# Attention sum of a GRU recurrence: from the exponential's own sum to a second ScalarE pass, with its products inside the gate products

## What is computed

```python
def step(h, x_t):
    proj = h @ W
    score = jnp.einsum('bsh,bh->bs', enc_hiddens, proj)     # 77 context rows
    attn = jax.nn.softmax(score, axis=-1)
    context = jnp.einsum('bs,bsh->bh', attn, enc_hiddens)
    inp = jnp.concatenate([x_t, context], axis=-1)
    gx = inp @ kernel + bias
    gh = h @ recurrent_kernel
    z = jax.nn.sigmoid(xz + hz)
    r = jax.nn.sigmoid(xr + hr)
    cand = jnp.tanh(xh + r * hh)
    h_new = z * h + (1.0 - z) * cand
    return (h_new, h_new)
```

## Time and profile before

| | |
|---|---|
| median of 3 runs | 3198.2 us (3195.73 to 3201.64) |
| the profiled execution | 3192.87 us, its span 3190.7 us |
| mean granted TensorE clock | 0.967 of full |
| TensorE products, weight loads | 2753.8 us (86%), 1822.2 us (57%) |
| VectorE | 2173.4 us (68%) |
| ScalarE | 1711.2 us (54%) |
| GpSimd | 931.2 us (29%) |
| first and last exponential of the recurrence | 1035.1 and 3021.4 us from the start |

### The profile page before, as it was taken

One profiled execution on the slowest core, in us unless ns is written; L12 is line 12 of the kernel. 1 busy time (PEld: TensorE's weight loads), 2 busy tenths in 40 slices (PEclk: granted clock), 3 DMA queues, 4 the chain that ended last, 5 costly groups with the idle time before them and its releaser, 6 DMA issues. The chain is left out here.

```text
span 3190.7 us, 131407 instructions
## 1 busy us (share of the span) xinstructions
PE 2753.8 (86%) x54380; PEld 1822.2 (57%) x54382; DVE 2173.4 (68%) x8164; ACT 1711.2 (54%) x5751; POOL 931.2 (29%) x1930
## 2 busy tenths in 40 slices
PE   5999999787678999898999898999989777777769
PEld 3666666575445555565665565666556444444449
DVE  5666666773442888688888787777778766666663
ACT  3666666533443666575776575666667433333311
POOL 0000000030010566354666354555535200000011
PEclk8999999998888999999999999999999999999979
DMA  4000000000011000010000010000000000000012
GB/s 137 5 5 5 7 5 5 1 1 10 16 32 41 7 14 30 3 43 4 10 14 27 16 31 3 10 10 12 21 17 23 3 4 3 3 3 3 3 46 61
DMA packets 38727, 55.45 MB, mean 17 GB/s; under 512 B 5934, under 2 KB 25336, under 8 KB 38008
## 3 DMA queue, kind: packets, MB, share of 16 engines
q1 hardware_dynamic: 36344, 42.46, 4.3%
q0 software_dynamic: 1792, 4.62, 0.6%
HBM read 42.45 MB, written 4.62 MB: 15 GB/s over the span
## 5 line engine op out<-in xcount | busy, mean ns | idle before, releaser
L2016 POOL TENSOR_TENSOR gru_terms<-gru_states,gru_signs 128x8 f32<-128x8 f32 x512 | 103.6, 202 | 1196.5 <-DVE gru_states L2222 1088.5
L1937 ACT ACTIVATE gru_p<-gru_ps_sg,gru_negmax 128x78 f32<-128x78 f32 x512 | 166.9, 326 | 361.2 <-DVE gru_negmax L2191 356.2
L1941 ACT ACTIVATE gru_th_r<-gru_pre_r 128x32 f32<-128x32 f32 x512 | 118.9, 232 | 408.7 <-DVE gru_pre_r L2202 408.7
L1576 PE MATMUL gru_ps_sg<-ctx_gate_w,gru_p_t 128*4 128x64 f32 x12288 | 267.4, 220 | 0.0
L343 ACT ACTIVATE self_probs<-self_sc,self_negmax 128x512 f32<-128x512 f32 x256 | 174.2, 684 | 166.2 <-DVE self_negmax L397 166.2
L1993 POOL TENSOR_SCALAR bg_probs<-bg_probs,bg_arsum 128x256 f32<-128x256 f32 (+2 forms) x192 | 240.5, 1253 | 19.0
L1778 PE MATMUL gru_ps_sg<-score_w,gru_states 128*4 128x78 f32 x4096 | 164.5, 233 | 93.0 <-DVE gru_states L2222 92.1
L2195 DVE STREAM_TRANSPOSE gru_p_t<-gru_p 128x96 f32<-128x96 f32 x512 | 142.6, 278 | 112.8 <-ACT gru_p L1937 112.7
L2191 DVE TENSOR_REDUCE gru_negmax<-gru_ps_sg 128x1 f32<-128x78 f32 x512 | 121.8, 238 | 133.4 <-PE gru_ps_sg L1778 129.7
L1782 PE MATMUL gru_ps_own<-late,gru_states 128*4 128x128 f32 x4096 | 207.1, 274 | 0.0
L2202 DVE SCALAR_TENSOR_TENSOR gru_pre_r<-gru_ps_sg,gru_rtotal,gru_own 128x32 f32<-128x32 f32 x512 | 127.3, 249 | 113.5 <-PE gru_ps_sg L1576 99.5
(11 more groups left out here) (392 smaller groups left out, 7367.0 us busy)
## 6 DMA issues: line engine op xcount, KB each, us to landing
bg_w<-in_moe_w SPq DMA_DIRECT2D x48, 256.0 KB, 3.3
bg_wa<-in_wqkv SPq DMA_DIRECT2D x24, 192.0 KB, 2.3
moe_w<-in_moe_w SPq DMA_DIRECT2D x16, 256.0 KB, 3.0
best_w_sb<-in_ec_w SPq DMA_DIRECT2D x16, 256.0 KB, 3.3
cross_scratch<-ctab_raw SPq DMA_DIRECT2D x16, 154.0 KB
cross_outs<-cross_scratch POOLq DMA_DIRECT2D x4, 576.0 KB, 6.0
late<-in_late SPq DMA_DIRECT2D x1, 2269.5 KB
self_w_sb<-in_wqkv SPq DMA_DIRECT2D x8, 192.0 KB, 2.4
```

Source lines behind the costliest of these rows:

```text
L1576: last = pe.matmul(bank[32 * c:32 * c + B, 0:hi - lo], p_t[:, 32 * k:32 * k + B], gate_w[:, k, 96 * c + lo:96 * c + hi], start=k == 0, sto ...
L1937: act.activation(p[:, 0:CTX + 1], ps_s[:, 0:CTX + 1], ACT.Exp, bias=negmax[:, 0:1], accum_out=total[:, 0:1])\
```

## The change

On ScalarE, the exponential no longer makes its sum. A wait for the exponential follows on ScalarE itself, then a copy of its 78 columns into a new tile `p_again` that is read by nobody and whose sum goes to `total`; a new semaphore `s_sum` tells of it. On TensorE, the 4 products of the sum leave their place ahead of the filler product and stand between the second and the third of the three parts of `ps_g`; they wait for `s_sum`. VectorE's list is unchanged.

```diff
@@ recurrence
-        p, p_t = sb("p", CPAD), sb("p_t", CPAD)
+        p, p_again, p_t = sb("p", CPAD), sb("p_again", CPAD), sb("p_t", CPAD)
@@
-            def gate_products(bank, lo, hi):
-                for k in range(3):
+            def gate_products(bank, lo, hi, chunks=range(3)):
+                for k in chunks:
@@ block.tensor
                 after_own(t)
-                pe.wait_ge(s_exp, t + 1)
+                pe.wait_ge(s_own, t + 1)
+                fill_in(P, ps_own)
+                pe.wait_ge(s_pt, t + 1)
+                gate_products(ps_g, 0, 64, range(2))
+                pe.wait_ge(s_sum, t + 1)
                 for c in range(4):
                     last = pe.matmul(ps_t[32 * c:32 * c + B, 0:2], spread, total[:], start=True, stop=True, tile_position=(0, 32 * c))
                 last.then_inc(s_total, 1)
-                pe.wait_ge(s_own, t + 1)
-                fill_in(P, ps_own)
-                pe.wait_ge(s_pt, t + 1)
-                gate_products(ps_g, 0, 64).then_inc(s_rcmm, 1)
+                gate_products(ps_g, 0, 64, range(2, 3)).then_inc(s_rcmm, 1)
                 pe.wait_ge(s_rt, t + 1)
                 gate_products(ps_z, 64, 96).then_inc(s_zmm, 1)
@@ block.scalar
                 act.wait_ge(s_max, t + 1)
-                act.activation(p[:, 0:CTX + 1], ps_s[:, 0:CTX + 1], ACT.Exp, bias=negmax[:, 0:1], accum_out=total[:, 0:1])\
-                   .then_inc(s_exp, 1)
+                act.activation(p[:, 0:CTX + 1], ps_s[:, 0:CTX + 1], ACT.Exp, bias=negmax[:, 0:1]).then_inc(s_exp, 1)
+                act.wait_ge(s_exp, t + 1)
+                act.activation(p_again[:, 0:CTX + 1], p[:, 0:CTX + 1], ACT.Copy, accum_out=total[:, 0:1]).then_inc(s_sum, 1)
                 after_exp(t)
```

More of the change, by code:

```diff
@@ L1433, in recurrence @@
         (s_init, s_load, s_table, s_score, s_ownmm, s_total, s_rcmm, s_zmm, s_max, s_exp, s_pt, s_rt, s_own, s_prer, s_thr, s_prez,
-         s_thz, s_u, s_cin, s_cand, s_tz, s_onez, s_tc, s_h, s_olds, s_hist) = (
+         s_thz, s_u, s_cin, s_cand, s_tz, s_onez, s_tc, s_h, s_olds, s_hist, s_sum) = (
             sem(n) for n in ("init", "load", "table", "score", "ownmm", "total", "rcmm", "zmm", "max", "exp", "pt", "rt", "own",
-                             "prer", "thr", "prez", "thz", "u", "cin", "cand", "tz", "onez", "tc", "h", "olds", "hist"))
+                             "prer", "thr", "prez", "thz", "u", "cin", "cand", "tz", "onez", "tc", "h", "olds", "hist", "sum"))
         h_cols, x, y, g_rows, b_rows, gain, bias, ident = (later[n] for n in (
```

## The result

The changed kernel takes 3342.4 us, the median of 4 runs (3339.54 to 3349.97), against 3197.0 of the kernel before in the same comparison (3194.42 to 3201.64): ratio 1.0458, interval 1.0445 to 1.0471. Forecast were 3311 and a range of 3281 to 3350: slower as forecast, within the range, with a loss of 145 us where the sum said 113.

A forecast was written before the change was run, and what follows sets the result against it. The recurrence's chain of waits between engines was taken to bound the kernel. Losses of 20 + 36 + 16 + 19 + 22 = 113 us on 3192.9 give 3306, plus 5 for the median: 3311 us, range 3281 to 3350.

The forecast's parts named there:

- the way of the sum stays free: Rival, chance 0.03: the exponential's 0.09 gain is kept and the sum's way costs nothing; 3178 us if all steps gained 0.04.
- other work hides the loss: Rival, chance 0.07: other waits already hold steps with VectorE background, so half of their 93 us falls away: 3265 us.
- the high bounds: Upper sizes of the terms: 0.15 in the 224 steps, 0.05 more in each other; 141 us lost, 3339 us.
- a late copy: Rival, chance 0.05: ScalarE's copy delivers the sum 0.05 behind its place in each step, 26 us more, 3337 us.
- a slow pace of the sum's products: Rival, chance 0.04: on TensorE the 8 records pace like gate products, 0.06 to 0.07 more a step, 3346 us.
- The place of the sum's products: On TensorE, the products start 0.91 after the exponential's start, behind two of three parts, instead of 0.47.
- The rival of eight starts 25 ns apart: Chance 0.01: the sum's products on TensorE queue singly, last start 0.18 behind the first, 0.13 more a step, 3378 us.
- The reciprocal, the first mis-sized term: On VectorE, the reciprocal starts 0.28 after the sum's products as now, so it runs from 1.20 to 1.37.
- Quiet steps: The 224 steps without VectorE background: `pre_r` at 1.40, only 0.03 late; 0.09 lost a step, 20 us.
- `c_in` "waiting no longer for `th_r`": In steps without VectorE background, `c_in` follows `pre_z` on VectorE, starting at 2.01 instead of 1.92.
- Expert steps: 96 steps with a background piece between reciprocal and `pre_r`: `pre_r` at 1.89 instead of 1.44; 0.38 a step, 36 us.
- The clock: Rival, chance 0.05: TensorE, less busy, loses its granted clock, some 0.5 a step over the last 150 steps: 3386 us.

The follow-up runs named there:

- freeing TensorE's queue: Changed kernel with the sum's products in another bank, so the `ps_z` products no longer wait for the reciprocal: 3328.8 us alone, ratio 1.0417.
- VectorE's order: Changed kernel with `ps_z` freed and `s_rt` listed first, plus VectorE's `hidden` and maximum pieces issued ahead of the reciprocal: 3260.5 us, ratio 1.0218.
- the first experiment: Changed kernel with the exponential making its own sum again and no copy; the sum's products stay between parts two and three: 3387.8 us, ratio 1.0585.
- second experiment: Changed kernel, copy kept, with the sum's products ahead of all gate products again: 3258.7 us, ratio 1.0183.
- the experiment on the order of the waits: Changed kernel with the three waits ahead of `pre_r` reordered so that `s_rt` is listed first: 3332.1 us, ratio 1.0414.
- the one with one part ahead: Changed kernel with `ps_z` freed and `s_rt` listed first, plus the sum's products behind one part of `ps_g` instead of two: 3262.8 us, ratio 1.023.
- the first mixture: The 3158 us version plus copy and later sum's products only in steps without VectorE work, `ps_z` free, gate products and reciprocal sharing a semaphore: 3183.0 us.
- the 3158 us version: Kernel before, without the change, with factors and transposed candidate raising one semaphore that the state's scan waits for first: 3158.0 us, ratio 0.9903.
- Both mixtures: The first mixture, 3183.0 us, and a second counting more steps as quiet, with the filler product behind the sum's products in another bank, 3207.0 us.

## Why the prediction was right, and where it was off

**The sign and its cause.** Forecast was that the late reciprocal holds two queues, VectorE's and TensorE's. The move alone costs more than the whole change; freeing TensorE's queue helps tile 2 and not the experts, and VectorE's order helps the experts. That is the stated mechanism, by kinds of step. It also answers the rivals in which the way of the sum stays free or other work hides the loss.

**The range.** The time lies within it by luck. The loss of 145 us is above the 141 of the high bounds; 3342 is inside only because the range was stretched to 3350 for a late copy and a slow pace of the sum's products, and neither came. (The chances that lie outside the range also add up to 0.22, not to 0.20 at most.)

**The exponential without its sum, +0.09 in hand.** Transposition at 0.36, as forecast; 0.09 a step by the first experiment.

**The copy.** 0.27, sum read by 0.72, no cost: right, and shown by taking it out. It is not late. ScalarE is 130 us busier, not 140.

**The place of the sum's products.** 0.91 forecast, 0.916 measured. The rival of eight starts 25 ns apart wanted the reciprocal 0.13 later than its 1.20; it came 0.035 later. The eight records again take 0.21 together and some 0.17 each, so the last starts some 0.04 behind the first. So the Trainium skill's floor for matmul starts ("TensorE: Matmul & The Clock Gate", section "Wait — 56ns, not 53.3ns?") is not seen for these products, of which four lie side by side. The rival of the slow pace wanted the third part 0.11 behind the sum's first record; it starts 0.06 behind it.

**The reciprocal, the first mis-sized term.** The step said "0.28 after them as now". It is 0.317 wherever gate products stand ahead of the sum's in TensorE's list, 0.280 where they don't (second experiment). That is 0.035 in every step, some 18 us over 512. It accounts for the +0.03 by which expert, tile 2's and the maxima's steps exceed their forecast. Why the result is later behind gate products is not shown.

**Quiet steps, the term most off.** "`pre_r` starts at 1.37 + 0.03 = 1.40, only 0.03 late": it started at 1.536. 0.035 is the reciprocal, 0.10 the queue instruction that the wait for `s_rt` is left to. Before, that wait ended at 0.92 and the instruction was long done when `ps_g` came; the change made its wait the last one. From `pre_r` the delay passes whole: it is 0.167 later, and the state 0.165. The term of 224 x 0.09 = 20 us was 37, 0.165 a step. The high bound of 0.15 also lay below: it counted delays of work, not the handing over of a wait. But the queue instruction is not the whole of the 0.075: with its price taken away by the order of the waits, quiet steps still lose 0.137 (3.897). So 0.028 needs it, and 0.047 is there without it, on the way by `pre_z`.

**`c_in` "waiting no longer for `th_r`"** was wrong: `th_r` ends at 2.05 and `c_in` starts 0.03 behind. The way by `pre_z`, which the forecast took for the later one, had been put too early, by 0.05 at `pre_z` (1.90, not 1.85), most of it the reciprocal's 0.035. It alone would have set `c_in` at 2.07 and not at 2.01, as the experiment on the order of the waits shows; the way by `pre_r` alone gives 2.08, as `ps_z` set free alone shows. The two are nearly tied, so that taking away either gives little.

**Expert steps**, 1.89 forecast and 1.93 measured for `pre_r`: right but for the reciprocal's term. There the background piece stands between, and the order of the waits changes nothing (4.31 with either), so the queue instruction's price is hidden.

**The clock.** From 2500 to 3160 it was granted in full, with TensorE busy 81%; columns as in the earlier trace rows:

```profile
2500.00:3160.00 660.00, 534.54 (x14769) 304.52 (x14771) 419.96 (x1883) 298.89 (x1230) 103.62 (x385) 1.00 0.02 6
```

**What the sum lacks.** It gave 113, the kinds of step 139, the span 147. 26 us are the two terms above and the roundings of tile 3; 5.3 lie behind the last exponential, where nothing was changed but the rest of the last step. Their cause is open, but they need not come from the change. That stretch takes 169.3 us in the kernel before and 174.7 in the changed one; it takes 167.0 to 169.5 in the four experiments on the chip with 3188.9, two of which hold the change, and 175.2 to 176.9 in the other eight. The 2 to 3 us between 139 and 141.7 are not accounted for by the medians.

## What to carry to other kernels

Before a producer is moved later in a chain, list every queue that waits for it and price each by what stands behind the wait; taking away one of two nearly tied waits gives little, so pair the edits. Look also at which wait of a consumer ends last: where several are listed, put the one that ends last on the instruction itself, here by listing it first, and look for gaps of 0.13 us between end and start on one engine. A small product inside a group of larger ones is as late as its place in the list, however little it costs.

## What was not expected of the hardware

- **A wait carried by the queue costs 0.10 us when it ends last.** `pre_r` follows the reciprocal by 0.134 with its wait in the queue instruction and by 0.035 with the wait on itself; the state's scan by 0.131 and 0.035. The Trainium skill ("Perfetto Trace Analysis", section "Identifying Dependency Chains") says that an instruction waiting for several engines may have EventSemaphore instructions put ahead of it; the trace agrees, with one of 50 ns in each of 512 steps. That the wait listed first is the one that rides on the instruction fits the four edits here that change which wait that is, and is not known beyond them.
- **The sum's result is 0.037 later behind larger products**, counted from its own first record: 0.317 in the changed kernel, the first experiment and the one with one part ahead, 0.280 in the kernel before and the second experiment. The cause is open.
- **A joint semaphore helps one waiter and can hurt another** that needed only half of it: the input products of the first mixture stood at 1.48, not 1.29. This was read from the timeline and not tested alone.
- **Still open:** whether the copy in quiet steps can add to the 3158 us version. Both mixtures gained 0.04 in quiet steps and lost more elsewhere; a version with quiet steps' gain and the others untouched was not run.
